# Handing the normalisation factors to all channels by SP transfers instead of TensorE in the two passes with an MLP

## What is computed

```python
xn  = (x - mean(x)) * rsqrt(var(x) + eps) * g1 + b1        # over the 96 channels
qkv = xn @ w_qkv + b_qkv
o   = softmax(q @ k.T * 16**-0.5) @ v                       # 6 heads of 16 channels
x1  = x + o @ w_proj + b_proj
xn2 = (x1 - mean(x1)) * rsqrt(var(x1) + eps) * g2 + b2
x2  = x1 + gelu(xn2 @ w_fc1 + b_fc1) @ w_fc2 + b_fc2        # 96 -> 384 -> 96
```

## Time and profile before

| | us |
|---|---|
| median of 3 runs (lowest to highest) | 11433.82 (11431.51 to 11441.5) |
| the profiled execution: its own time | 11434.82 |
| its span, from first to last instruction | 11433.0 |

### The profile page before, as it was taken

The page is one execution under the profiler, slowest core; times in us unless marked ns, Lnnn a source line. Parts: engine busy times, 40 slices in busy tenths (PEclk is TensorE's granted clock), DMA queues, the critical chain, the costliest instruction groups (busy, mean ns, idle before and its releaser), DMA issues. The chain is left out here.

```text
span 11433.0 us, 395055 instructions
## 1 busy us (share of the span) xinstructions
PE 10873.7 (95%) x160084; PEld 8530.3 (75%) x160084; DVE 7310.2 (64%) x12431; ACT 7647.9 (67%) x13429; POOL 5844.1 (51%) x7492
## 2 busy tenths in 40 slices
PE   6999998999999999999899999998999999999999
PEld 4666666777777777777677777776878778877877
DVE  4555555777777777763476767675666666666665
ACT  4555555777777777763376767675777777777776
POOL 2333334777777777760054444443555555555554
PEclk9999998999999999999999999998999999999999
DMA  2111111222222222226533333331110111011110
GB/s 60 50 46 50 49 40 38 52 51 52 52 51 52 51 51 52 52 49 212 179 81 77 79 77 79 77 80 29 24 25 24 24 25 24 24 25 24 25 24 21
DMA packets 1105566, 617.50 MB, mean 54 GB/s; under 512 B 864636, under 2 KB 1076551, under 8 KB 1099689
## 3 DMA queue, kind: packets, MB, share of 16 engines
q1 hardware_dynamic: 1091368, 552.46, 20.2%
q10 hardware_dynamic: 12288, 38.54, 1.0%
HBM read 307.18 MB, written 282.75 MB: 52 GB/s over the span
## 5 line engine op out<-in xcount | busy, mean ns | idle before, releaser
L1499 POOL TENSOR_TENSOR L_HdL<-L_Hd,L_HdH 128x392 fp32r<-128x392 f32 x1536 | 1573.0, 1024 | 280.8 <-POOL L_HdH L1497 280.1
L1006 PE MATMUL banks<-L_ident,L_PR 113*113 113x113 f32 x9216 | 1201.3, 267 | 1.2 <-DVE L_X L1405 0.7
L1006 PEld LDWEIGHTS banks<-L_ident,L_PR 113*113 113x113 f32 x9216 | 1142.9, 180 | 64.1 <-DVE L_X L1405 9.8
L1497 POOL CAST L_HdH<-L_Hd 128x392 fp32r<-128x392 f32 x1536 | 786.0, 512 | 737.7 <-issue 681.9
L1234 ACT COPY L_PT<-banks 113x452 f32<-113x452 f32 x1792 | 885.9, 538 | 398.7 <-PE banks L1006 398.2
L1250 ACT ACTIVATE L_PR<-L_SX 113x588 f32<-113x588 f32 x1536 | 1087.9, 708 | 51.7 <-DVE L_SX L1377 10.3
L1069 PE MATMUL banks<-L_VB,L_PT 113*49 113x34 f32 x36864 | 1064.0, 213 | 1.4 <-ACT L_PT L1234 1.0
L1277 ACT ACT_TABLE_LOAD x512 | 656.9, 1283 | 603.7 <-PE banks L1013 603.6
L1371 DVE TENSOR_REDUCE L_MX<-banks 113x12 f32<-113x588 f32 x1024 | 783.6, 765 | 432.0 <-PE banks L1052 432.0
L1488 POOL CAST L_XNH<-L_XN 97x392 fp32r<-97x392 f32 x512 | 448.5, 876 | 1159.9 <-DVE L_XN L1418 1159.9
L1069 PEld LDWEIGHTS banks<-L_VB,L_PT 113*49 113x49 f32 x36864 | 1015.9, 126 | 24.9 <-issue 1.5
(11 more groups left out here) (249 smaller groups left out, 28424.8 us busy)
## 6 DMA issues: line engine op xcount, KB each, us to landing
L_X<-after_L SPq DMA_DIRECT2D x768, 147.0 KB
after_L<-L_X SPq DMA_DIRECT2D x512, 147.0 KB
conv_T<-L_norm_by_phase SPq DMA_DIRECT2D x96, 512.0 KB, 3.3
L_norm_by_phase<-L_XP SPq DMA_DIRECT2D x512, 84.0 KB, 2.1
scan_XT<-in_x SPq DMA_DIRECT2D x32, 1176.0 KB, 7.1
L_norm<-L_XA SPq DMA_DIRECT2D x256, 147.0 KB, 1.9
L_conv<-conv_D ACTq DMA_DIRECT2D x96, 392.0 KB, 3.0
L_XR<-L_norm SPq DMA_DIRECT2D x256, 147.0 KB, 2.4
```

Source lines behind the costliest of these rows:

```text
L1006: mm = pe.transpose(bank(TURN[a])[0:SPAN, (k % 4) * SPAN:(k % 4 + 1) * SPAN], PR[:, st.v if lag else st.u, 2 * k:2 * k + 2, :].rearrange(" ...
L1497: pool.tensor_copy(HdH[:, u, j].bitcast(F32R), Hd[:, u, j]).then_inc(s[f"hd_high_{j}"], 1)
L1499: pool.tensor_tensor(HdL[:, u, j].bitcast(F32R), Hd[:, u, j], HdH[:, u, j], ALU.subtract).then_inc(s[f"hd_parts_{j}"], 1)
```

## The change

In the MLP passes `spread` moves from PE to SP: one DMA per normalisation copies its 32 factor rows three times over, into the 96 rows of a new SBUF tile RB, and `normalised` multiplies with RB instead of PSUM. SP does so at the start of its step, ahead of the load of chunk t+2. PICK, the semaphore `spread` and NORM_BANK are gone. Around it: SQ2 is computed on DVE, as the last operation of its step, instead of on ACT; the second half of the softmax's exponential moves to ACT's next step, behind `rstd`; the residual comes behind both halves of maximum and subtraction; VB's odd values come ahead of `normalised`; on PE `variances` comes ahead of all three outputs, turn 0 behind them, and `scores` ahead of `hidden`; ACT loads the GELU table ahead of its wait for `hidden 0`.

```diff
@@ PE, variances and spread @@
-                    if kind == "L1":
-                        st.wait("xh", 5)
-                    else:
+                    st.wait("lv", 0)
+                    if kind == "L3":
                         st.wait("y", 4)
...
-                def spread(st):
-
-                    st.wait("rstd", -1)
-                    for k in range(PAIRS):
-                        cols = slice(2 * TOK * k, 2 * TOK * (k + 1))
-                        for g, _ in norms(st):
-                            rows = slice(NORM_ROWS * g, NORM_ROWS * (g + 1))
-                            mm = pe.matmul(bank(NORM_BANK[g])[0:C, cols], PICK[rows], RS[rows, st.u, cols], start=True, stop=True)
-                    mm.then_inc(s["spread"], 1)
@@ SP @@
+                def spread(st):
+
+                    present = [g for g, there in enumerate((st.ahead().f, st.m, third_norm(st))) if there]
+                    if present:
+                        st.wait("rstd", -1)
+                    for g in present:
+                        rows = RS[NORM_ROWS * g:NORM_ROWS * (g + 1), st.u].unsqueeze(1)
+                        sp.dma_start(RB[:, g, st.u], rows.broadcast_to([NORM_ROWS, C // NORM_ROWS, CH])).then_inc(spread_rows[g][st.u], 16)
...
                 def step(st):
+                    if mlp:
+                        spread(st)
@@ PE, mlp_step @@
                         st.wait("gelu_1", 3)
+                    if normed:
+                        variances(st)
+                    if st.n:
                         output(st, 0)
                         output(st, 1)
+                        output(st, 2).then_inc(s["fc2"], 1)
                     if st.k:
                         st.wait("probs0", 1)
                         turn(st, 0)
-                    if normed:
-                        variances(st)
-                    if st.n:
-                        output(st, 2).then_inc(s["fc2"], 1)
-                    if st.k:
...
-                    if normed:
-                        spread(st)
...
                     if st.k:
                         heads(st)
+                    if st.f:
+                        scores(st)
                     if st.m:
                         st.wait("xn2_parts", 2)
...
-                    if st.f:
-                        scores(st)
@@ ACT, mlp_step @@
                     if st.k:
+                        probs(st, 1, 1)
                         pt_copy(st, 1)
                         pt_copy(st, 2)
...
                     if st.m:
+                        act.preload_act_table_set(GELU)
...
-                    if st.k:
-
-                        st.wait("variances", 0)
-                        st.wait("x1", 1)
-                        act.activation(SQ2[:, st.v], x1_of(st, 1)[0:C], ACT.Square).then_inc(s["sq2"], 1)
-                    if st.f:
-                        probs(st, 1, 0)
@@ DVE, normalised @@
-                    st.wait("spread", -1)
                     if st.m:
-                        dve.tensor_tensor(XN2[0:C, st.u], x1_of(st, 2)[0:C], bank(NORM_BANK[1])[0:C, 0:CH], ALU.mult).then_inc(s["xn2"], 1)
+                        st.wait_turn(spread_rows[1][st.u], 2, 1)
+                        dve.tensor_tensor(XN2[0:C, st.u], x1_of(st, 2)[0:C], RB[:, 1, st.u], ALU.mult).then_inc(s["xn2"], 1)
...
@@ DVE, mlp_step @@
                     if st.f:
                         keys(st)
+                    if st.f:
+                        values_odd(st)
                     if normed:
                         normalised(st)
-                    if st.f:
-                        values_odd(st)
                     if st.k:
                         over_sums(st)
                     if st.f:
                         centre(st, 0)
+                        centre(st, 1)
                     if st.k:
                         residual(st)
-                    if st.f:
-                        centre(st, 1)
+
+                        st.wait("variances", 0)
+                        st.wait("x1", 1)
+                        dve.tensor_tensor(SQ2[:, st.v], x1_of(st, 1)[0:C], x1_of(st, 1)[0:C], ALU.mult).then_inc(s["sq2"], 1)
```

More of the change, by code:

```diff
@@ L749, in window_pass @@
         if mlp:
-            J = sb("J", [C, NORM_ROWS]); PICK = sb("PICK", [C, C])
+            J = sb("J", [C, NORM_ROWS]); RB = sb("RB", [C, 3 if kind == "L1" else 2, 2, CH])
             SQ = sb("SQ", [C, 2, CH]); SQ2 = sb("SQ2", [C, 2, CH]); LV = sb("LV", [C, 2, CH]); RS = sb("RS", [C, 2, CH])
@@ L793, in window_pass @@
             loads += [(gb[:, 0:1], column(p["dw_b"]))]
-        load_all(nc, kind, loads, zeros=zeros, values=[(J[:], 1.0 / C), (PICK[:], 0.0)] if mlp else [])
+        load_all(nc, kind, loads, zeros=zeros, values=[(J[:], 1.0 / C)] if mlp else [])
         with nc.Block() as block:
@@ L802, in _ @@
                     dve.memset(eps[:], EPS)
-                    for g in range(C // NORM_ROWS):
-                        dve.memset(PICK[NORM_ROWS * g:NORM_ROWS * g + 1], 1.0)
                 if kind == "L3":
@@ L843, in window_pass @@
             names += ["xn_high", "xn_parts", "xn2_high", "xn2_parts"]
-            names += ["sq", "sq2", "variances", "lv", "rstd", "spread", "xn2", "fc2", "x2"]
+            names += ["sq", "sq2", "variances", "lv", "rstd", "xn2", "fc2", "x2"]
             names += [f"fc1_{j}" for j in range(HB)] + [f"gelu_{j}" for j in range(HB)]
@@ L858, in window_pass @@
         phases_stored = [sem(f"phases_stored{u}") for u in range(2)] if kind == "L1" else []
+        spread_rows = [[sem(f"spread{g}{u}") for u in range(2)] for g in range(3 if kind == "L1" else 2)] if mlp else []
         passed = sem("passed")
@@ L867, in window_pass @@
         K_BANK, Q_BANK = (7, 3) if mlp else (3, 6)
-        VAR_BANK, NORM_BANK = 2, (0, 1, 2)
+        VAR_BANK = 2
         TOKEN_BANK = (2, 6)
@@ L955, in _ @@
                     load(Step(sp, s, c, c, True), 0)
+                if mlp:
+                    spread(Step(sp, s, -1, -1, True))
                 over_chunks(sp, s, step, LAST)
@@ L1040, in scores @@
                     else:
-                        if st.ahead().f:
-                            st.wait("xn", -1)
-                        if third_norm(st):
-                            st.wait("xh", 4)
+                        st.wait("lv", -1)
                         if kind == "L3" and st.n:
@@ L1210, in _ @@
                     variances(first)
-                    spread(first)
                 over_chunks(pe, s, mlp_step if mlp else attention_step, LAST)
@@ L1216, in _ @@
                 LOG_EXP = "natural_log_exp_and_others"
+                GELU = "gelu_and_others"
                 def rstd(st):
@@ L1227, in rstd @@
                     st.wait("lv", -1)
+                    for g in present:
+                        st.wait(("xn", "xn2", "xh")[g], (1, 4, 6)[g])
                     for rows in parts:
@@ L1258, in mlp_step @@
                     if st.k:
+                        probs(st, 1, 1)
                         pt_copy(st, 1)
                         pt_copy(st, 2)
+                    if st.f:
+                        values_even(st)
                     if st.m:
@@ L1412, in normalised @@
                     nx = st.ahead()
-                    st.wait("spread", -1)
                     if st.m:
-                        dve.tensor_tensor(XN2[0:C, st.u], x1_of(st, 2)[0:C], bank(NORM_BANK[1])[0:C, 0:CH], ALU.mult).then_inc(s["xn2"], 1)
+                        st.wait_turn(spread_rows[1][st.u], 2, 1)
+                        dve.tensor_tensor(XN2[0:C, st.u], x1_of(st, 2)[0:C], RB[:, 1, st.u], ALU.mult).then_inc(s["xn2"], 1)
                     if nx.f:
                         nx.wait_turn(loaded[nx.of4(0)], 0, N_LOADS, 4)
-                        dve.tensor_tensor(seen(XN[0:C, nx.u]), win(X[0:C, nx.of4(0)]), win(bank(NORM_BANK[0])[0:C, 0:CH]), ALU.mult).then_inc(s["xn"], 1)
+                        nx.wait_turn(spread_rows[0][st.u], 0, 1)
+                        dve.tensor_tensor(seen(XN[0:C, nx.u]), win(X[0:C, nx.of4(0)]), win(RB[:, 0, st.u]), ALU.mult).then_inc(s["xn"], 1)
                     if st.m:
@@ L1425, in normalised @@
                         st.wait("xa", 6)
-                        dve.tensor_tensor(XH[:, st.u], X2[0:C, st.u], bank(NORM_BANK[2])[0:C, 0:CH], ALU.mult).then_inc(s["xh"], 1)
+                        st.wait_turn(spread_rows[2][st.u], 4, 1)
+                        dve.tensor_tensor(XH[:, st.u], X2[0:C, st.u], RB[:, 2, st.u], ALU.mult).then_inc(s["xh"], 1)
                 def mlp_step(st):
```

2 lines of the change are left out of this document (removed).

## The result

| | before | changed |
|---|---|---|
| median (range) | 11433.11 us (11431.51 to 11441.5, 4 runs) | 12389.78 us (12371.1 to 12399.79, 4 runs) |
| ratio | 1 | 1.0834 (95% interval 1.0817 to 1.085) |
| L1 pass, first to last copy of turn 0 | 3274.1 us | 4089.9 us |
| L3 pass, the same | 3551.0 us | 3728.5 us |
| TensorE clock, L1 and L3 | 0.99 and 0.99 | 0.89 and 0.99 |

A forecast was written before the change was run, and what follows sets the result against it. The prediction took PE to bound both passes before, and POOL's loop to decide L1 afterwards. It summed 857 (L1) + 60 (L3) - 40 (loop starts) = 877 on 11435 us, 12310, named 12290, range 11670 to 12500.

The forecast's parts named there:

- POOL's chain decides: L1: late X and the port put POOL's loop at about 16.0 us a step against 12.62, 857 us more.
- A: The start of DVE's copy of turn 0, from which the forecast counts the times within a step.
- the price of the port: L1: five DVE operations with two SBUF inputs and POOL's SBUF reads exclude each other; seven operations queue for 4.4 us.
- Its parts on SP: L1, load of X: three DMA issues at 0.4 us each, X landing 3.1 us after its first issue.
- DVE's loop without port and DMA: SQ2, variances, outputs, turn 0, copy, back to SQ2: 3.1 us on PE plus 10.1 on DVE, 13.2 us.
- three waits: L3, on PE: turn 2 0.35, scores 0.15, variances 0.9 us; step 14.0 us, 60 us more in all.
- The start of the loop, -40: At every pass of the loop PE idles longer; part of this disappears into its slack, minus 40 us.
- the port costs little: Rival: DVE's and POOL's reads fall beside each other, X's load decides L1 at 14.1 us; total 11690, chance 0.17.
- Slow transfers: Rival: factor transfers on SP take 4 us each instead of about 2.6; total about 12870, chance 0.08.
- PE stays the bound: Rival: both passes get faster with PE still limiting; minus 440 us at full price, 10995; chance 0.05.

The follow-up runs named there:

- psum_operand: The changed kernel, but XN2, XN and XH inside the hardware loops multiply by a PSUM bank instead of the SBUF factors; 12156.48 us, ratio 1.0628.
- load_first: The changed kernel, but SP issues the load of X ahead of the factor transfers; 11943.08 us, ratio 1.0445.
- turn_first: load_first, but PE transposes turn 0 ahead of the variances instead of behind the nine output matmuls; 11890.0 us, ratio 1.0401.
- warm: The changed kernel with queries, turn 0 and scores done over again on PE in its L1 waits, results the same; 12334.83 us, ratio 1.0791.

## Why the forecast held, and where it did not

- **PE stops being the bound in L1, and POOL's chain decides**: right in the main. Over 240 steps of L1 PE waits for HdL in 173, but in 122 also for SQ2, by 1.06 us, so DVE's loop, held up at the same port, has its part. X lands 6.8 us after the variances (forecast 6.6), A + 2.4 (2.6); XNL starts at A + 6.7 and A + 5.8 in the two steps shown (7.0); HdL 2 ends at A + 14.5 (15.0); the next copy 1.27 later (1.25). That makes 15.7 in the step shown and 15.28 on average at full clock, instead of 16.0. The mis-sized term is the price of the port: the forecast's step was 14.1 without it and 16.0 with it, 1.9 us, and psum_operand shows 0.7 for three of the five operations.
- **Its parts on SP**: one factor transfer takes 0.63 us to issue (1.90 for three), not 0.4, and X lands 2.56 us after the start of its issue, not 3.1. The two errors nearly cancel.
- **The clock**: left out. L1's 816 us are 3.20 a step: 2.65 at full clock and 0.55, about 140 us, in the steps with dips, which the kernel before hardly has. The forecast had 3.4 a step without a clock, so L1 came out by cancelling, and that is luck.
- **DVE's loop without port and DMA**: forecast 13.2, measured 14.2 in load_first (L1). From the copy to SQ2's end it is 10.4 (10.1 with the hand-over), and from the variances to the copy 3.7 where I had 3.1, of which output 2's wait for HdL is 0.36. Its rank in L1 was right: it is the second bound there.
- **L3**: forecast +60 us, measured +178. The mechanism held: PE's own step with three waits put in. Two of them have the size forecast, on average 0.32 us ahead of turn 2 (forecast 0.35, where its own terms give 0.29) and 0.85 ahead of the variances (0.9). The third is mis-sized: the scores wait for Y in every step, by 0.50 on average, not 0.15. At full clock the step rose by 0.56, not 0.25, about 140 us. The rest is mainly the nine steps where the loop starts again, 3.6 us longer each, 32 us; dips elsewhere add next to nothing.
- **The start of the loop, -40**: wrong in sign. What the nine steps take over a full-clock step fell by 0.8 us each in L1 and rose by 3.0 in L3 with the second stop, together about +20 us. The -29 us measured outside the passes are another thing, which the forecast called unchanged.
- **The total**: 12390 against 12290. L1 is 41 us under its term and L3 118 over.
- **Rivals**: "the port costs little" had the loop through X at 14.1; psum_operand, without the factors' port, is at 14.5, and the durations of 0.83 to 1.20 us contradict its premise. "Slow transfers": the factor transfers landed 2.6 us after issue in the median, so no. The Trainium skill, "DMA: Bandwidth & Descriptors", "Anatomy of one DMA", gives 2.3 by a fit for DMAs that GpSimd issues; SP issues these, and the measurement decides. "PE stays the bound" is excluded by PE's 77% at full clock in L1 and by the waits above.

What stays open: why the clock falls. In steps of L1 at full clock PE is idle (the step less its busy time) 3.5 us in the changed kernel, 2.5 in load_first and 1.8 in turn_first, and 118 of 230, 8 of 215 and 66 of 218 steps have a lower clock: neither the busy share nor the idle time puts them in order. What the traces do show is where it falls: in L1 of the changed kernel, 107 of 120 falls have as PE's last wait before them the one for XN2L ahead of hidden 0 or the next, for the heads' quotients O. These two take 1.16 and 0.44 us there, 0.73 and 0.41 in turn_first (52 of 60 falls), and 0.36 and 0.38 in load_first, whose nine falls all belong to starts of the loop. But in psum_operand 37 of 64 falls follow the wait for SQ2, so this is no rule, and no run changed one of these waits alone. The Trainium skill, "TensorE: Matmul & The Clock Gate", "HAM oscillation — how this bites in real kernels", lays such oscillation to waits of the matmul stream, in a kernel that waits longer than it computes in each turn of its loop; here the longest wait in L1 of the changed kernel outside the starts of the loop is 1.9 us, against 11.8 us of work. warm, which fills waits, agrees that they matter.
